# A long convolution on one Trainium2 core: odd states finished ahead of the next channel's pairs on VectorE, and the states' high part copied ahead of the inputs on ScalarE

## The reference, cut to what matters

```python
# x: (64, 128, 2048) = batch, channel, time; N = 64 states a channel
u_m  = u * mask[:, None, :]                         # mask[b, t] = t < length[b]
K    = 2.0 * einsum('hn,hnl->hl', Cs, exp(P)).real  # P = dtA * arange(2048)
y    = irfft(rfft(u_m, 4096) * rfft(K, 4096))[..., :2048]
y    = y + u_m * D[:, None]
return x + y * mask[:, None, :]
```

## Time and profile before

| | |
|---|---|
| median of 3 runs | 896.73 us (895.91 to 896.87) |
| profiled execution, its own time | 895.97 us |
| its span, first to last instruction | 894.0 us |
| busy: TensorE, VectorE, ScalarE, GpSimd | 95%, 81%, 76%, 67% |
| granted TensorE clock, mean of the core | 1.000 |

### The profile page before, as it was taken

The page is one execution under the profiler, slowest core; times in us unless marked ns, Lnnn a source line. Parts: engine busy times, 40 slices in busy tenths (PEclk is TensorE's granted clock), DMA queues, the critical chain, the costliest instruction groups (busy, mean ns, idle before and its releaser), DMA issues.

```text
span 894.0 us, 23094 instructions
## 1 busy us (share of the span) xinstructions
PE 847.8 (95%) x6299; PEld 776.9 (87%) x6299; DVE 721.7 (81%) x2043; ACT 680.2 (76%) x1717; POOL 598.5 (67%) x847
## 2 busy tenths in 40 slices
PE   0789999999999999999999999999999999999997
PEld 0778999989898998989989899898999989899896
DVE  7967887888878888788888878888788887888886
ACT  4677777777777787777777777777777777778784
POOL 5975766676666767667676676766667676676763
PEclk9999999999999999999999999999999999999999
DMA  4155777677666666666666666666666666666774
GB/s 103 48 125 135 194 185 186 175 185 180 176 190 168 186 180 180 186 170 188 175 184 182 173 184 176 185 182 174 185 173 186 181 176 189 168 186 179 188 184 130
DMA packets 161553, 153.69 MB, mean 172 GB/s; under 512 B 13688, under 2 KB 161272, under 8 KB 161400
## 3 DMA queue, kind: packets, MB, share of 16 engines
q1 hardware_dynamic: 161224, 153.14, 64.2%
q10 hardware_dynamic: 304, 0.26, 0.1%
HBM read 84.02 MB, written 67.30 MB: 169 GB/s over the span
## 4 chain that ended last, share of the span: by engine, by line
PE 88%; DVE 3%; issue 2%; POOL 2%; ACT 2%; DMA 1%; SPq 0%; DVEq 0%; POOLq 0%
PE y L1133 15%; PE y L1135 13%; PE y L1134 13%; PE y L1181 12%; PE v L1133 9%; PE xt_even L1118 6%; PE xt_odd L1118 6%; PE v L1134 6%; PE v L1135 6%; PE y L1129 1%; PE y L1128 1%; ACT room L602 1%; DMA xall<-in_x_dram 1%; POOL uol L570 1%; PE y L1277 0%
## 5 line engine op out<-in xcount | busy, mean ns | idle before, releaser
L602 ACT ACTIVATE room<-v 64x192 f32<-64x192 f32 (+1 forms) x768 | 235.8, 307 | 67.0 <-PE v L1135 54.9
L986 DVE SCALAR_TENSOR_TENSOR mid<-room,RV,v 128x192 f32<-128x192 f32 (+2 forms) x512 | 182.5, 357 | 63.4 <-ACT room L602 63.1
L570 POOL TENSOR_TENSOR uol<-uod,uoh 128x448 fp32r<-128x448 f32 x85 | 98.1, 1155 | 165.1 <-ACT uod L602 165.1
L986 DVE SCALAR_TENSOR_TENSOR v<-v,RV,mid 128x192 f32<-128x192 f32 (+2 forms) x512 | 177.6, 370 | 16.5
L1133 PE MATMUL y<-thi,uhi 128*128 128x256 f32 x511 | 185.9, 364 | 0.3 <-POOL tlo L539 0.3
L975 DVE COPY_PREDICATED xall<-mask,y 128x512 f32<-128x512 int32 x254 | 176.4, 744 | 0.0
L551 POOL TENSOR_TENSOR room<-W,B 128x256 f32 (+1 forms) x254 | 157.8, 621 | 23.4 <-POOL room L560 11.0
L1133 PE MATMUL y<-fhi,zhi 128*128 128x256 f32 x511 | 153.9, 301 | 2.0 <-DVE zlo L1039 2.0
L1039 DVE SCALAR_TENSOR_TENSOR zlo<-v,RV,zhi 128x448 fp32r<-128x448 f32 x128 | 87.5, 684 | 76.5 <-ACT zhi L749 76.5
L1135 PE MATMUL y<-thi,ulo 128*128 128x256 f32 x511 | 144.5, 283 | 0.0
L1135 PE MATMUL y<-fhi,zlo 128*128 128x256 f32 x511 | 144.2, 282 | 0.0
(11 more groups left out here) (227 smaller groups left out, 2012.5 us busy)
## 6 DMA issues: line engine op xcount, KB each, us to landing
xall<-in_x_dram SPq DMA_DIRECT2D x256, 256.0 KB, 4.3
out_dram<-xall SPq DMA_DIRECT2D x254, 256.0 KB, 3.3
traw<-krows SPq DMA_DIRECT2D x128, 128.0 KB, 2.9
NXY<-B SPq DMA_DIRECT2D x2, 512.0 KB, 6.0
W<-W SPq DMA_DIRECT2D x2, 480.0 KB, 6.0
krows<-ksb SPq DMA_DIRECT2D x8, 1.0 KB, 2.0
krows<-ksb SPq DMA_DIRECT2D x8, 4.0 KB, 3.8
krows<-ksb SPq DMA_DIRECT2D x8, 11.0 KB, 3.8
```

Of the source, the lines that this page charges most:

```text
L570: pool.tensor_tensor(uol[j % 2][:], uod[j % 3][:, 0:EVERY], uoh[j % 2][:].bitcast(F32), ALU.subtract).then_inc(s_uol, 1)
L602: return act.activation(dst, src, ACT.Copy)
L986: return dve.scalar_tensor_tensor(out=out, in0=src, scalar=RV[:, k:k + 1, h], in1=other, op0=ALU.mult, op1=ALU.add)
```

## The change: the diff

On VectorE `odds(*here)` now stands right behind `odds_turned(*here)`, and `x_low`, `e_low` each move ahead of one scan step. On ScalarE `z_high(*here)` now stands ahead of `x_high(*two)`, and `x_odd(*two)` ahead of `turn_pairs(*one)`. No instruction is added or taken away.

```diff
@@ scalar, slot @@
+                z_high(*here)
                 if has2:
                     x_high(*two)
-                z_high(*here)
+                    x_odd(*two)
                 if has1:
                     turn_pairs(*one)
                 if has2:
-                    x_odd(*two)
                     e_high(*two)
@@ vector, slot @@
                 odds_turned(*here)
+                odds(*here)
                 if has1:
                     pairs_turned(*one)
-                odds(*here)
-                if has1:
                     pairs(*one)
                 z_low(*here)
+                if has2:
+                    x_low(*two)
                 if has1:
                     fours_turned(*one)
                 if has2:
-                    x_low(*two)
+                    e_low(*two)
                 if has1:
                     fours(*one)
-                if has2:
-                    e_low(*two)
-                if has1:
                     sixth(*one)
```

## The result

The changed kernel takes **883.44 us** (882.88 to 884.54, 4 runs), the kernel before 896.48 (895.91 to 896.87, 4 runs): a ratio of 0.9857, interval 0.9839 to 0.9874, or 13.0 us less. The forecast was 882.8.

The account below looks back on a forecast made before the run. A ring through all four engines was taken to hold the period at 6.55 us; 108 x (6.445 - 6.55) = -11.3 and -2.6 in written-out channels make -13.9, so 896.73 becomes 882.8 us, range 877 to 893.

Parts of the forecast that it names:

- The new ring: ScalarE and VectorE, from `zhi` through `turn_pairs`, `elo`, `fours` and `odds` to the next `zhi`: period 6.445 us in the loop.
- `odds_turned` to `odds`: Dependent neighbours on VectorE: 0.55 us from start to start, where independent neighbours take 0.33.
- the written-out channels: Some 12 channels outside the loop, without register steps: period from 6.34 to about 6.12 us, -2.6 us in total.
- TensorE's own work: Period less TensorE's two gaps, 6.55 - 0.26 - 0.17: 6.12 us a channel.
- A wait of `fours_turned`: On VectorE: a new wait for `room` of about 0.35 us ahead of `fours_turned`.
- A gap of about 0.35 ahead of `odd_sums`: On TensorE: `odd_sums` still starts late, with a gap of about 0.35 us ahead of it.
- A: VectorE's dependent links cost nothing, TensorE's 6.12 us binds everywhere: about 847 us; chance 0.03.
- B: `elo` starts 0.14 behind `ehi`, not 0.03; period 6.55, only written-out channels gain: about 894 us; chance 0.05.
- C: ScalarE's hand-overs `zhi`-`uhi` and `uhi`-`uod` don't overlap; period 6.71 us: slower, about 912 us; chance 0.07.
- D: Another unseen ring is at 6.55 us: no change, about 896 us; chance 0.07 together with half of C.
- The joint of two prices: On ScalarE, `zhi` to `uhi`: overlap of 0.10 to 0.11 us taken; a start 0.02 behind the end was the alternative.
- the ring that was cut: Through all four engines, `zhi` by `uoh`, `uol`, `odd_sums`, `turn_odds`, `pairs_turned`, `odds` to `zhi`: 6.55 us, the old period.

Follow-up runs that it names:

- after_two_groups: Changed kernel with two groups of six channels in each turn of the hardware loop: 878.63 us, ratio 0.9814 to the kernel before.
- odds_only: Kernel before with only `odds` moved ahead of `pairs_turned` on VectorE: 845.56 us, ratio 0.943 to the kernel before.
- odds_unrolled: Kernel before with only `odds` moved ahead of `pairs_turned` and the hardware loop written out: 841.31 us, ratio 0.9386 to the kernel before.
- pairs_early: Changed kernel with ScalarE's `x_odd` moved behind `turn_pairs` and `e_high`: 860.69 us, ratio 0.9595 to the kernel before.
- lows_stay: Changed kernel with `x_low` and `e_low` left in their old places: 920.74 us, ratio 1.0269 to the kernel before.
- the pad: Unused 64-column addition put ahead of `choose` on VectorE: changed kernel 916.63 us, kernel before 897.95 us, kernel with `odds` alone moved 863.17 us.

## Why the prediction was right, step by step

**The new ring, right.** From `zhi` at 465.00 the steps came at 0.53 (`uhi`; predicted 0.52), 1.01 (1.01), 1.64 (1.63), 2.22 (`ehi`; 2.21), 2.64 (`elo`; 2.62), 2.98 (`fours`; 2.95), 3.47 and 3.90 (`sixth`; 3.44, 3.85), 5.38 (`odds_turned`; 5.33), 5.82 (`odds`; 5.88), and 6.39 (next `zhi`; 6.445). Each joint is within 0.03 of its price but one. The prediction speaks of two pairs of full-height neighbours in the earlier trace rows; they show one (49.82 to 50.09), and the other is in the earlier trace rows.

**`odds_turned` to `odds`, mis-sized.** "From `odds_turned` to `odds` it is then 0.40 + 0.15 = 0.55": it is 0.44 (470.38 to 470.82). I priced it by `sixth`, where a register step stands between the wait and the instruction. Between 470.40 and 470.82 the trace has none, as `odds` needs no new register value there; in the slot in which the loop turns it has one (53 ns, at 484.0), and the pair takes 0.54 (483.54 to 484.08). So in five slots of six the ring has three links with a register step and not four, and this link is 0.11 shorter than predicted; the slot takes 6.38 to 6.43.

**The turn of the loop, left out.** I took the period as the same in all slots. VectorE's branch, its register work and the start of the next instruction add 0.34 between `sixth` and `choose` (0.55 in place of 0.21), and the register step ahead of `odds` 0.10, together 0.44: the slot of 6.82. The same branch stood in the kernel before and cost nothing, since VectorE then waited 0.54 ahead of `pairs_turned`. A slot of the kernel before in which the loop turned:

```profile
447.22 0.29 DVE L986 SCALAR_TENSOR_TENSOR v<-v,RV,mid 128x64 f32<-128x64 f32 x1
447.76 0.06 DVE L974 MEMSET tick<- 128x1 f32 x1 [0.25 <-issue]
...
449.65 0.42 DVE L986 SCALAR_TENSOR_TENSOR mid<-room,RV,v 128x192 f32<-128x192 f32 x1 [0.19 <-ACT room L602]
```

There 0.19 of that wait was left even so. The two terms have opposite signs: (5 x 6.39 + 6.82)/6 = 6.46, against 6.445. That the sum came out near is in part luck, and `after_two_groups` shows the second term by itself. A further term of the same kind was left out: the step into the loop took 7.31 (127.84 to 135.15), where the kernel before had 6.57 (129.41 to 135.98). It took 6.55 in `after_two_groups`, and no run shows the cause. The loop gave 701.2 - 691.9 = 9.3 us (11.3 predicted), the rest of the span, 894.0 - 882.7 - 9.3 = 2.0, is what was left of the gain in the written-out channels (2.6 predicted).

**TensorE's own work, 6.12 predicted, 6.06 found.** I took the wait ahead of `odd_sums` off the period, but not what follows a wait: the first matmul behind it takes 0.28 to the next (469.47 to 469.75), where 0.20 is the pace. `odds_only` shows the work without that, 6.06 a slot. It did not enter the sum for the loop. For the written-out channels it did: they were to be at 6.12 by TensorE's work and were at 6.16 in the mean, in turns of 6.05 and 6.26. They are not at TensorE's bound, since `odds_unrolled` reaches 6.06. What makes them alternate was not worked out.

**The signs.** Idle time ahead of `zhi` as before, released by `v`: yes. A wait of `fours_turned` of about 0.35: 0.28. No wait of `from_state`: yes. A gap of about 0.35 ahead of `odd_sums`: 0.23, and 0.08 more behind it.

**The rivals.** A (dependent links are free) falls with `odds` 0.44 behind `odds_turned` where independent neighbours of that length take 0.33, and 6.39 instead of 6.06 as the period. The sentence of the Trainium skill (VectorE: DVE Perf Modes, The DRAIN you can't avoid) on the semaphore was measured there on a row of copies; for this pair, in which the second instruction waits for the first, it is off by 0.11. B falls with `elo` 0.03 behind `ehi`, C with `uhi` at 0.53 and not at 0.66. D falls with the period of 6.39, and with `pairs_early` and `lows_stay`, in which steps of the new ring alone were moved and the time went by -22.8 and +37.3. The joint of two prices came out at 0.11 and 0.12 of overlap.

**What I did not ask.** The prediction priced the change as a whole and was right about it; that its best part would be 845.56 by itself could have been asked of the same rows, because without `uhi` and `uod` the ring of ScalarE and VectorE is, by an estimate from the rows after, 6.39 - 0.97 = 5.42, shorter than TensorE's work.

## What to carry to other kernels

In a pipeline written out by hand, list the rings through the in-order engines and add up each: the period is the longest, and a change is worth the distance to the next longest. A copy that stood in an engine's waiting time can come to lie on the longest ring once it is moved behind the instruction that was waited for: here two copies of about 0.48 cost 75 us, more than the ring that was cut had given. A short instruction on unused data, put on one engine, shows room where its cost vanishes. Where it costs time, look at its own row first: here it waited for another engine and made a ring that was not there before.

## What the runs showed of the hardware

- In a hardware loop, an instruction whose address or wait needs a fresh register value starts 0.14 after its input is ready (483.94 to 484.08), one that needs none 0.04 (470.78 to 470.82). The two instructions of `sixth` stand 0.43 apart in the loop of the kernel after (468.47 to 468.90) and 0.32 in its written-out channels (855.03 to 855.35).
- The addition on VectorE with both inputs in SBUF, put in as the pad, ended 0.07 to 0.15 after the GpSimd instruction that was running when it began, in every slot of the loop of three kernels. Its length was 0.22 to 0.69 for the same 64 columns.
- A turn of the loop costs VectorE 0.34 us of start-to-start time, though its compare and branch is 56 ns long (the row below, of the kernel after). The Trainium skill (Advanced Engine Details and Errata, Control Flow Timing) has about 108 ns for a compare-and-branch; neither figure is what a ring loses.

```profile
L260 DVEq COMPARE_BRANCH  x18: 50/56/67, 171.4 to 831.0; - x18
```

- With all channels written out the same order gained 31.0 us (883.44 to 852.41), and the kernel before 23.4 (896.33 to 872.96), with nothing else changed.
- In `odds_only` most of the first 20 slots of the loop are longer than the rest (6.14 to 6.84), and the written-out kernels have a few single slots of 6.3 to 7.0. The cause stays open.
